# Fetching blocks of x with indirect gathers from GpSimd instead of plain transfers from SyncE

## The chip, the cores and the metric

The kernel runs on one core of a Trainium2 chip. The metric is the device time in microseconds (us) of one execution. A profile is one further execution, seen by the hardware profiler; its times are counted from the first instruction of its span. The engines are named as in the profile: PE is TensorE (PEld its weight loads), DVE is VectorE, ACT is ScalarE, POOL is GpSimd, SP is SyncE.

## What is computed

x has 16 blocks of 512 nodes with 128 features. A graph step and a mixture-of-experts step follow each other, each with a layer norm and a residual:

```python
def _layernorm(x): ...                      # over the last axis
def gnn(x):                                 # x is layernorm(x)
    h = x @ fc_in_w.T + fc_in_b
    for _ in range(8):
        h = h + 1/8 * (sigmoid(alpha) * 0.5 * (adj @ h - h) + h @ w_eff - h + x)
    return h
def moe(t):                                 # t is layernorm(x)
    p = softmax(t @ router_w.T)             # 8 experts, the 2 best, renormed
    return t + sum_e combine[:, e] * (gelu(t @ w1[e] + b1[e]) @ w2[e] + b2[e])
x = x + gnn(layernorm(x))
x = x + moe(layernorm(x))
```

## The kernel before

The 16 blocks are worked through as 8 groups of two blocks (GB = 2). The eight Euler steps are one polynomial in the node matrix and the feature matrix, worked out once at the start (up to about 57 us). Every fp32 operand of a matrix product is split in a high part (written by ACT) and a low part (written by DVE or POOL), and each product is three matmuls of these parts, `mm3`, lines 954 to 956.

Each engine has its own program, with semaphores between them. A loop body for group g holds two things: the graph step of group g, and after it the expert stage of group g - 1, with the first products of group g + 1 at its end. The first group has no expert stage (`iteration(0, first=True)`), then comes a hardware loop over groups 1 to 6, then `iteration(7, final=True)` and a last expert stage alone.

The expert stage has ITEMS = 16 items: two blocks by eight experts. Item i goes through the engines in this order: PE multiplies by w1 (the "up" product), ACT takes the gelu (line 494), DVE scales it by the routing weight (line 818, into `scaled`), ACT writes the high part into `scs` (line 397), POOL writes the low part (`item_low`, line 348), and PE multiplies by w2 (the "down" product), LAG = 5 items behind the up product. `scaled` has three slots, so DVE scales item i only after the low part of item i - 3 (line 817). `scs` has RING = 6 slots. Four of the 16 low parts, items 3, 4, 8 and 15 (`LOW_DVE`), are DVE's; the other 12 are POOL's. In the same stage DVE takes the statistics of the second layer norm (items 1 to 3), POOL takes the inverse root after item 2 (`inverse_root`, line 337), and DVE writes the normed z (line 579, items 6 to 8). PE transposes z at items 11 and 12.

POOL's order in a loop body: `residual(g - 1)` (line 355), the inverse root of the first layer norm of group g + 1, the sum of Q and xg (line 372), two low parts of x0 (line 342), then the low parts of the items with one inverse root among them. In the first group there are no items, and `residual(0)` is the next body's first instruction. DVE waits for it (`res_ready`, line 888) before its first sum of line 893.

x comes in as 256 KB transfers, one for each block of a group, into the one buffer `xn`. SP's `next_x(g)` waits until group g - 1 has been normed (`x0_ready`) and copied to `xg` (`xg_copied`), then issues two transfers (line 252). In a loop body it stands behind the replicated routing rows (`expert_weights`, line 286) and ahead of the stores of results (`store`, line 262). The data are read first by DVE's statistics of line 561 at the start of the next body.

## Time and profile before

| what | value |
|---|---|
| runs of the kernel before | 621.85 and 626.67 us, median 624.26 us |
| span of the profiled execution | 619.0 us |
| mean granted TensorE clock in it | 0.983 of full speed |
| length of one loop body | about 69.3 to 70.5 us, six of them |
| expert stage in it (group 3's body) | from 267.1 us to about 298.6 us |

The profile gives the span alone of the profiled execution, not its device time. The median of the runs is 5.3 us above the span, the two runs 2.9 and 7.7 us above it. Three views of the profile are used below. The timeline lists the instructions of one engine in order: start, duration, engine, line, operation, output<-input, and in brackets the idle time of the engine before it with what ended it. A group row ("x12 | 19.4, 1643") gives a count, the busy time in us and the mean of one in ns. A row by tile or line gives the shortest, median and longest duration in ns. An instruction's duration begins when it is issued to the engine, so that it holds time in which it is blocked.

### The profile page before, as it was taken

The numbers are of one execution on the slowest core, as the hardware profiler recorded it, in microseconds if no ns is written. First come the engines' busy times: TensorE is split into PE (matmuls) and PEld (weight loads), VectorE is DVE, ScalarE is ACT, GpSimd is POOL, SyncE is SP. The second block draws the span as 40 slices with busy tenths as digits, with TensorE's granted clock in tenths as the row PEclk, the third lists the DMA queues.
The fourth block names the chain that finished last, engine by engine and source line by source line (L and its number), as shares of the span: only waits on it lengthen the run. The fifth ranks groups of instructions, "written<-read, shape, count | busy, mean of one in ns | idle before, by whom it ended". The sixth has DMA issues, their size and how long they took to land.

```text
span 619.0 us, 9553 instructions
## 1 busy us (share of the span) xinstructions
PE 566.9 (92%) x3023; PEld 481.9 (78%) x3023; DVE 473.5 (76%) x1090; ACT 290.9 (47%) x477; POOL 250.2 (40%) x155
## 2 busy tenths in 40 slices
PE   3999999998999799998999799998999799998796
PEld 2778988976898588976898588976898588976574
DVE  5799776779676976779676976779676985579666
ACT  4322131367415662367415662367415672257574
POOL 2230320447213751447313761447313761147355
PEclk9999999999999999999999999999999989998899
DMA  5100010360105200250105300360105200350141
GB/s 181 35 0 1 0 35 1 107 202 1 34 2 210 95 17 17 104 203 0 34 2 197 107 17 17 104 203 0 34 2 191 80 17 19 104 171 0 43 164 35
DMA packets 25759, 43.15 MB, mean 70 GB/s; under 512 B 1462, under 2 KB 20236, under 8 KB 23820
## 3 DMA queue, kind: packets, MB, share of 16 engines
q1 hardware_dynamic: 25740, 42.91, 20.9%
q8 instruction: 10, 0.16, 0.1%
q14 instruction: 9, 0.07, 0.0%
HBM read 38.45 MB, written 4.46 MB: 69 GB/s over the span
## 4 chain that ended last, share of the span: by engine, by line
PE 63%; DVE 20%; issue 9%; ACT 3%; POOL 2%; DMA 1%; DVEq 0%; POOLq 0%; SPq 0%; ACTq 0%
PE bank L954 19%; PE bank L956 18%; PE bank L955 18%; DVE work L818 6%; DVE scr L579 3%; DVE bn L561 2%; PE bank L1080 2%; DVE scs L557 2%; POOL scs L348 2%; DVE x L579 2%; ACT work L494 2%; DVE mv L567 1%; PE bank L973 1%; PE bank L1094 1%; DMA work<-in_adj_dram 1%
## 5 line engine op out<-in xcount | busy, mean ns | idle before, releaser
L348 POOL TENSOR_TENSOR scs<-work,scs 128x512 fp32r<-128x512 f32 x96 | 153.1, 1617 | 103.5 <-ACT scs L397 103.3
L397 ACT ACTIVATE scs<-work 128x512 fp32r<-128x512 f32 (+1 forms) x129 | 82.8, 642 | 53.6 <-DVE work L818 52.3
L494 ACT ACTIVATE work<-bank,cols 128x512 f32<-128x512 f32 x128 | 86.8, 679 | 27.3 <-PE bank L956 27.0
L818 DVE TENSOR_TENSOR work<-work,GT 128x512 f32<-128x512 f32 x90 | 87.9, 990 | 9.6 <-ACT work L494 8.9
L337 POOL TENSOR_TENSOR rstd<-ve,nhalf 128x8 f32<-128x8 f32 x16 | 29.7, 1856 | 113.6 <-DVE ve L575 113.6
L954 PE MATMUL bank<-M,GT 128*128 128x384 f32 x192 | 65.6, 342 | 0.1
L955 PE MATMUL bank<-M,GT 128*128 128x384 f32 x192 | 65.0, 339 | 0.0
L956 PE MATMUL bank<-M,GT 128*128 128x384 f32 x192 | 65.0, 338 | 0.0
L557 DVE TENSOR_TENSOR GT<-bank,GT 128x512 fp32r<-128x512 f32 x48 | 32.2, 687 | 38.3 <-ACT GT L397 38.3
L954 PE MATMUL bank<-scs,w2s 128*128 128x512 f32 x128 | 56.3, 440 | 4.4 <-DVE scs L557 2.7
L397 ACT ACTIVATE GT<-bank 128x512 fp32r<-128x512 f32 x48 | 27.7, 594 | 67.5 <-PE bank L956 63.3
L397 ACT ACTIVATE scs<-Q 128x512 fp32r<-128x512 f32 x16 | 10.1, 632 | 94.1 <-DVE Q L893 94.1
L954 PE MATMUL bank<-LT,x0s 128*128 128x512 f32 x128 | 52.2, 408 | 1.8 <-DVE x0s L557 1.6
L954 PE MATMUL bank<-zT,w1s 128*128 128x512 f32 x128 | 53.8, 420 | 0.0
L955 PE MATMUL bank<-zT,w1s 128*128 128x512 f32 x128 | 51.8, 404 | 0.0
L956 PE MATMUL bank<-zT,w1s 128*128 128x512 f32 x128 | 51.7, 404 | 0.0
L955 PE MATMUL bank<-scs,w2s 128*128 128x512 f32 x128 | 51.4, 401 | 0.0
L956 PE MATMUL bank<-scs,w2s 128*128 128x512 f32 x128 | 51.3, 401 | 0.0
L956 PE MATMUL bank<-LT,x0s 128*128 128x512 f32 x128 | 51.3, 401 | 0.0
L893 DVE TENSOR_TENSOR Q<-bank,bias 128x384 f32<-128x384 f32 x64 | 35.5, 556 | 20.3 <-PE bank L956 19.5
L955 PE MATMUL bank<-LT,x0s 128*128 128x512 f32 x128 | 51.0, 398 | 0.0
L954 PE MATMUL bank<-scs,LT 128*128 128x256 f32 x128 | 36.7, 287 | 7.9 <-DVE scs L557 7.9
(188 smaller groups left out, 1382.1 us busy)
## 6 DMA issues: line engine op xcount, KB each, us to landing
GT<-comb_rows SPq DMA_DIRECT2D x8, 1536.0 KB, 6.8
Q<-comb_rows SPq DMA_DIRECT2D x16, 512.0 KB, 5.8
GT<-comb_rows SPq DMA_DIRECT2D x7, 1024.0 KB, 6.2
xn<-in_x_dram SPq DMA_DIRECT2D x16, 256.0 KB, 7.6
out_dram<-outs SPq DMA_DIRECT2D x16, 256.0 KB, 2.2
GT<-comb_rows SPq DMA_DIRECT2D x7, 512.0 KB, 4.3
work<-in_adj_dram SPq DMA_DIRECT2D x4, 256.0 KB, 5.4
Q<-in_L_ffn_w_dram SPq DMA_DIRECT2D x2, 512.0 KB, 5.9
```

The source lines that it names most:

```text
L337: nc.gpsimd.tensor_tensor(rstd[:, n, :], ve[:, n, :], nhalf[:, :], ALU.pow).then_inc(ln_rstd[n], 1)
L348: nc.gpsimd.tensor_tensor(scs[:, i % RING, 1, :], scaled[:, i % 3, :], scs[:, i % RING, 0, :].bitcast(FP32), ALU.subtract).then_inc(sc_lo_ ...
L397: return nc.scalar.activation(dst, src, ACT.Copy)
L494: nc.scalar.activation(hid[:, i % 2, :], bank[UP_BANK[i % 3]][:, :], ACT.Gelu, bias=cols[:, B1_COL + e:B1_COL + e + 1]).then_inc(gelu_done, 1)
L557: return v.tensor_tensor(dst, src, hi.bitcast(FP32), ALU.subtract)
L561: v.bn_stats(bn[:, n, t, :], src[:, t // GB, t % GB, :]).then_inc(ln_own[n], 1)
L579: return v.tensor_scalar(dst[:, t // GB, t % GB, :], src[:, t // GB, t % GB, :], mv[:, n, 0, t:t + 1], rstd[:, n, t:t + 1], ALU.subtract, ...
L818: v.tensor_tensor(scaled[:, i % 3, :], hid[:, i % 2, :], bank[REP_BANK[i % 2]][:, :] if by_pe else rep(i), ALU.mult).then_inc(sc_ready, 1)
L893: v.tensor_tensor(Q[:, :, t, b, :], src, bias[:, t], ALU.add).then_inc(q_ready, 1)
L954: pe.matmul(dst, wh, xh, start=start, stop=False)
L955: pe.matmul(dst, wh, xl, start=False, stop=False)
L956: return pe.matmul(dst, wl, xh, start=False, stop=stop)
```

## The change

All groups from 2 to 7 are fetched by POOL. Groups 0 and 1 still come by SP's plain transfers. A table of row numbers `x_row` (one column for each of the 8 tiles of 128 rows of a group) is written at the start; each `gather_x` is one indirect DMA that fetches 128 rows of 512 bytes, one to a partition, so a group is 8 gathers. In the first group all 8 stand behind the inverse root of line 337. In the loop bodies of groups 1 to 5 one stands behind each even item (0, 2, ..., 14), and behind item 0 there are also the addition that moves `x_row` on by a group (`next_rows`) and the two waits that were SP's. The body of group 6 is taken out of the loop, without gathers. DVE's statistics wait for the gathers' own semaphores.

```diff
@@ -86,6 +86,8 @@
+        x_row = sb("x_row", [P, NT, GB], I32)
+        x_step = sb("x_step", [P, NT, GB], I32)
@@ -164,6 +166,8 @@
+        rows_landed = [sem(f"rows_landed{b}") for b in range(GB)]
+        row_ready, gather_go = sem("row_ready"), sem("gather_go")
@@ -307,10 +311,8 @@
             next_x(1)
-            next_x(2)
             with sp.Fori(1, GROUPS - 2) as g:
                 expert_weights(g - 1, g)
-                next_x(g + 2)
                 store(g - 1)
@@ -329,7 +331,10 @@
             nc.gpsimd.memset(nhalf[:, :], -0.5).then_inc(pool_own, 1)
-            pool.wait_ge(pool_own, 2)
+            nc.gpsimd.iota(x_row[:, :, :], pattern=[[P, NT], [N, GB]], base=2 * GB * N,
+                           channel_multiplier=1)
+            nc.gpsimd.memset(x_step[:, :, :], GB * N).then_inc(pool_own, 1)
+            pool.wait_ge(pool_own, 3)
@@ -347,6 +352,25 @@
+            def next_rows(g):
+
+                for b in range(GB):
+                    pool.wait_ge(rows_landed[b], 16 * NT * (g - 2))
+                nc.gpsimd.tensor_tensor(x_row[:, :, :], x_row[:, :, :], x_step[:, :, :], ALU.add).then_inc(row_ready, 1)
+
+            def gather_x(g, k):
+
+                b, t = k // NT, k % NT
+                if k == 0:
+                    pool.wait_ge(x0_ready, g)
+                    pool.wait_ge(xg_copied, g)
+                    if not isinstance(g, int):
+                        pool.wait_ge(row_ready, g - 2)
+                    pool.sem_inc(gather_go, 1)
+                nc.gpsimd.indirect_dma_start(
+                    out=xn[:, t, b, :], out_offset=None, in_=x.rearrange("b n c -> (b n) c"),
+                    in_offset=bass.IndirectOffsetOnAxis(ap=x_row[:, t, b:b + 1], axis=0)).then_inc(rows_landed[b], 16)
@@ -362,7 +386,7 @@
-            def iteration(g, first=False, final=False):
+            def iteration(g, first=False, final=False, more=False):
@@ -374,16 +398,23 @@
                 if first:
                     inverse_root(1, g)
+                    for k in range(T):
+                        gather_x(g + 2, k)
                 else:
                     for i in range(ITEMS):
                         if i not in LOW_DVE:
                             item_low(g - 1, i)
                         if i == 2:
                             inverse_root(1, g)
+                        if more and i % 2 == 0:
+                            if i == 0:
+                                next_rows(g + 2)
+                            gather_x(g + 2, i // 2)
 
             iteration(0, first=True)
-            with pool.Fori(1, GROUPS - 1) as g:
-                iteration(g)
+            with pool.Fori(1, GROUPS - 2) as g:
+                iteration(g, more=True)
+            iteration(GROUPS - 2)
             iteration(GROUPS - 1, final=True)
@@ -580,7 +611,10 @@
             def norm_x_stats(g, b):
-                dve.wait_ge(x_in[b], 16 * g + 16)
+                if isinstance(g, int) and g < 2:
+                    dve.wait_ge(x_in[b], 16 * g + 16)
+                else:
+                    dve.wait_ge(rows_landed[b], 16 * NT * (g - 1))
```

## Rows read from the trace of the kernel before

**Rows 1.** Page, part 1: busy time, share of the span, instructions of each engine

```profile
PE 566.9 (92%) x3023; PEld 481.9 (78%) x3023; DVE 473.5 (76%) x1090; ACT 290.9 (47%) x477; POOL 250.2 (40%) x155
```

**Rows 2.** One body by stretches: length, PE, PEld, DVE, ACT, POOL busy, clock, DMA

```profile
239.00:270.20 31.20, 30.20 (x196) 28.80 (x196) 22.23 (x63) 11.04 (x19) 6.62 (x4) 1.00 0.25 89
270.20:296.50 26.30, 22.93 (x112) 17.25 (x111) 25.31 (x43) 19.27 (x33) 21.53 (x13) 1.00 0.22 75
296.50:309.00 12.50, 12.50 (x57) 10.09 (x56) 7.46 (x21) 4.75 (x9) 2.41 (x1) 1.00 0.14 42
```

**Rows 3.** Timeline of POOL in the expert stage: start, us, instruction, idle before

```profile
270.24 1.29 POOL L348 TENSOR_TENSOR scs<-work,scs 128x512 fp32r<-128x512 f32 x1 [9.30 <-ACT scs L397]
271.49 1.76 POOL L348 TENSOR_TENSOR scs<-work,scs 128x512 fp32r<-128x512 f32 x1
...
275.78 2.14 POOL L337 TENSOR_TENSOR rstd<-ve,nhalf 128x8 f32<-128x8 f32 x1 [0.83 <-DVE ve L575]
...
286.35 1.61 POOL L348 TENSOR_TENSOR scs<-work,scs 128x512 fp32r<-128x512 f32 x1 [1.94 <-ACT scs L397]
...
294.69 1.73 POOL L348 TENSOR_TENSOR scs<-work,scs 128x512 fp32r<-128x512 f32 x1
303.87 2.41 POOL L355 TENSOR_TENSOR scr<-Q,scr 128x1024 f32<-128x1024 f32 x1 [7.45 <-DVE outs L806]
```

**Rows 4.** Timeline of PE's weight loads: first and later down products, z's transposes

```profile
271.59 0.19 PEld L954 LDWEIGHTS bank<-scs,w2s 128*128 128x128 f32 x1 [0.27 <-POOL scs L348]
...
273.30 0.19 PEld L954 LDWEIGHTS bank<-scs,w2s 128*128 128x128 f32 x1 [0.47 <-POOL scs L348]
...
285.06 0.42 PEld L1094 LDWEIGHTS bank<-ident,scr 128*128 128x128 f32 x4 [3.10 <-DVE scr L579]
...
297.24 0.19 PEld L954 LDWEIGHTS bank<-scs,w2s 128*128 128x128 f32 x1
```

**Rows 5.** DVE: groups within 270.2 to 296.5, then shortest, median, longest over the span

```profile
L818 DVE TENSOR_TENSOR work<-work,GT 128x512 f32<-128x512 f32 x10 | 10.1, 1019 | 0.2 <-ACT work L494 0.2
L579 DVE TENSOR_SCALAR scr<-Q,mv,rstd 128x128 f32<-128x128 f32 x8 | 5.2, 699 | 0.0
...
L567 DVE TENSOR_TENSOR mv<-bn 128x8 f32<-128x8 f32 x1 | 1.3, 1259 | 0.0
...
L818 DVE TENSOR_TENSOR work<-work,GT x90: 674/693/1789, 129.0 to 606.3; 128x512 f32<-128x512 f32 x90
...
L579 DVE TENSOR_SCALAR x<-xn,mv,rstd x64: 335/341/2453, 10.6 to 464.3; 128x128 f32<-128x128 f32 x64
```

**Rows 6.** The transfers of x: SP's issue, and on the page KB and landing

```profile
268.45 1.06 SPq L252 DMA_DIRECT2D xn<-in_x_dram  x2
...
xn<-in_x_dram SPq DMA_DIRECT2D x16, 256.0 KB, 7.6
```

**Rows 7.** POOL: cheapest instruction, low parts of 270.2 to 296.5, inverse root

```profile
L331 POOL MEMSET nhalf<- 128x8 f32 x1 | 0.1, 102 | 0.0
...
L348 POOL TENSOR_TENSOR scs<-work,scs 128x512 fp32r<-128x512 f32 x12 | 19.4, 1643 | 13.1 <-ACT scs L397 13.1
...
L337 POOL TENSOR_TENSOR rstd<-ve,nhalf x16: 1642/1658/2138, 7.3 to 554.8; 128x8 f32<-128x8 f32 x16
```

**Rows 8.** Timelines of POOL, then DVE, behind the first group; last row a later body

```profile
86.96 1.65 POOL L337 TENSOR_TENSOR rstd<-ve,nhalf 128x8 f32<-128x8 f32 x1 [8.76 <-DVE ve L575]
90.98 2.36 POOL L355 TENSOR_TENSOR scr<-Q,scr 128x1024 f32<-128x1024 f32 x1 [2.37 <-DVE scr L579]
...
88.65 2.14 DVE L579 TENSOR_SCALAR scr<-Q,mv,rstd 128x128 f32<-128x128 f32 x8 [0.56 <-POOL rstd L337]
...
101.44 1.65 DVE L561 BATCH_NORM_STATS2 bn<-xn 128x6 f32<-128x128 f32 x8 [0.23 <-DVE rm L780]
...
103.60 0.55 DVE L893 TENSOR_TENSOR Q<-bank,bias 128x384 f32<-128x384 f32 x1
...
309.15 1.64 DVE L561 BATCH_NORM_STATS2 bn<-xn 128x6 f32<-128x128 f32 x8
```

## The prediction

> **What bounds the kernel now.** I read the page's busy times first. PE is busy 92% of the span and POOL 40% [rows 1]. That suggests that POOL has room, but it is an average over stages. The table by stretches shows where POOL's work lies: in a body of 70 us, 21.53 of its 30.56 us of busy time fall in the 26.30 us of the expert items, where it is 82% busy. DVE is busy 25.31 us of the same stretch and PE 22.93 [rows 2]. The gathers go into exactly this stretch.
>
> The timelines show who paces it. POOL's low part of item 0 ends at 271.53, and PE's waiting down product starts at 271.59. The next ends at 273.25, and PE starts at 273.30 [rows 3, 4]. So at its start POOL releases PE item by item. In the middle POOL idles briefly: 0.83 us for DVE before the inverse root, and 13.1 - 9.3 = 3.8 us for ACT before low parts [rows 3, 7], together about 4.65 us. PE waits 3.10 us for DVE's z [rows 4]. From 286.35 to 296.42 POOL works without a pause. Its last low part, item 14, ends at 296.42, and PE's down product of item 14 starts at 297.24 [rows 3, 4], only 0.82 us later.
>
> Last, I compared durations. A low part takes 1.29 us where it stands alone and 1.61 to 1.76 us where others precede it [rows 3]. DVE's scaling with two SBUF inputs takes 674 ns at best and 1,019 ns on average here; z's 128x128 scaling takes 699 ns on average here, where the same operation takes 335 ns elsewhere, and once 2,453 ns [rows 5]. Line 567, on 8 columns, took 1,259 ns [rows 5]. POOL and DVE hold each other up. DVE's excess is about (1.02 - 0.68) x 14 + (0.70 - 0.34) x 8 + 1.1 = 8.8 us per body.
>
> **What is removed.** SP's issue of 1.06 us per group, and a wait. SP next waits for stores that come much later, and nobody waits for x: its 7.6 us landing is over by about 277, and it is first read at 309.15 [rows 6, 8]. The removed part gives 0.
>
> **What is added, in a body with gathers.** POOL gets one addition on 128x8 integers, a few waits that are satisfied by then (SP's transfers, behind the same two waits, went out at 268.45 [rows 6]) and 8 gathers. The gather behind item 14 is followed by `residual`, which comes at 303.87 after 7.45 us of idling [rows 3], so it is hidden. Behind the other seven are queued low parts or the inverse root, which DVE's next scaling (through the three slots of `scaled`) and PE's down product wait for.
>
> The price D of one gather is the unknown: no POOL transfer is in this trace. From below there is POOL's cheapest instruction, 0.10 us [rows 7]. SP's issue of two larger transfers takes 1.06 us, so 0.53 each [rows 6]. From above there is the inverse root on only 8 columns, 1.66 to 2.14 us [rows 7], which shows what POOL's software costs where each element needs many steps. A gather reads 128 row numbers and writes out 128 rows' addresses by software, so I put it nearest to an undisturbed low part, D = 1.3 us [rows 3]. For the range I keep 0.1 and 2.1.
>
> The Trainium skill, "DMA: Bandwidth & Descriptors", section "Latency and other measured facts", puts GpSimd's first byte at about 1 us against 0.6 us for SyncE's. No row here shows it. By D = 1.0 the sum below would give about +2 us instead of +15.
>
> **The sum for one body.** I start at the end of item 0's low part, 271.53, and lay POOL's work end to end, since with gathers it has almost no pause left. The addition takes 0.2. Of the 11 low parts left, six follow a gather or one and meet DVE less (a gather gives DVE time): 6 x 1.29 = 7.7. Five follow another low part: 5 x 1.72 = 8.6. The inverse root takes 2.1. Seven gathers take 7 x 1.3 = 9.1. That is 27.7 us, and item 14 ends at 299.2 in place of 296.4. PE took it at 297.24, so PE is 2.0 us later. To this I add 0.5 us for pauses that stay (between 0 and the 4.65 us of idling there are now), most of the old idle time being filled. The result is +2.5 us per body. In this sum one tenth of a microsecond in D is 0.7 us per body. At D = 0.95 the whole is hidden.
>
> Everything behind item 14 (out, the first products of the next group, the next body) follows PE, so the 2.5 us aren't given back. PE, 87% busy in the stretch, can't make them up. Five bodies give 5 x 2.5 = 12.5 us.
>
> **The first group.** Eight gathers start at 88.6 and take 10.4 us, to 99.0. `residual` is queued behind them and moves from 90.98 to 99.0, ending at 101.4 [rows 8]. DVE needs it at 103.60, a cover of 2.2 us that is gone at D = 1.57. The last rows must land for the second half of DVE's statistics at 102.3 (101.44 plus half of 1.65). With the quickest landing of x in the trace (2.6 us) they come at 101.6. DVE's eight scalings of z start at 88.65 [rows 8], just when the gathers start, and may be blocked as above. I add 1.5 us for the group, between 0 and 8 (each scaling behind one gather at worst). The rest costs nothing: the two new setup instructions are as small as the cheapest row [rows 7] and stand at the start, where POOL waits for DVE's first statistics.
>
> Sum: 12.5 + 1.5 = 14, with half a microsecond of loop and semaphore instructions on POOL about 15 us. The profiled span would go from 619.0 to 634, and the median of runs, 5.3 us above the span, from 624.3 to 639.
>
> **Rivals.** *The gathers are hidden* (chance 0.30). If D is about 1.1 us or less, POOL's old pauses and its blocked time take them in. For it speaks that POOL idles 4.65 us in the stretch and is blocked for about 12 x (1.643 - 1.29) = 4.2 us [rows 7]. Against it speaks that seven gathers at 1.1 are 7.7 us and that the end has 0.82 us of slack. It gives 5 x (0 to 1) = 0 to 5 us, so 621 to 630.
>
> *The gathers cost more than a low part, or shut DVE out* (0.25). DVE is 96% busy in the stretch, and the line 579 rows show that it can be held for a whole POOL instruction. At D = 1.8 the sum gives 7 x 0.5 = 3.5 us more per body, and 2.1 + 2.4 - 2.2 = 2.3 us more in the first group: 639 + 17.5 + 2.3 = 659. At 2.1 it gives 5 x 5.6 + 6 = 34 more, 673.
> The Trainium skill, "SBUF — State Buffer", section "SBUF: two separate sides", warns of this pair: while DVE runs a copy or scaling in its two-port mode, GpSimd can't write descriptors, and it advises SyncE's path for such transfers. The rows agree that the two exclude each other, 2,453 ns for 335; how a gather fares no row shows. By that rule eight scalings of z per body lengthen gathers by up to 8 x 0.34 = 2.7 us, so up to 13 us in all, about 652.
>
> *Faster* (0.03). DVE is the busiest engine of the stretch and loses 8.8 us to POOL. If gathers are cheap (below about 0.5 us, so that 7 x 0.5 fits in the old pauses) and leave DVE's inputs alone, they spread the low parts and DVE's scalings run unblocked. The bound is PE's idle time of the stretch, 26.30 - 22.93 = 3.4 us per body, so at most 5 x 3.4 = 17 us: 607. Against it: the low parts stay as many and as long, and only a third of the cover would appear.
>
> *x comes late* (0.02 alone). The last gather would go out at about 299.2 to 300.5 and is needed, shifted by the same delay, at 311. It would need over 10 us to land, where 512 KB now take 7.6 [rows 6]. Then DVE would wait, and the next products behind it: over 3 us a body.
>
> **How the numbers follow.** The forecast, D of 1.1 to 1.6 and POOL pacing the items, has 0.40 and spans 630 to 652. The likeliest value is 639. The range leaves out the dearest part of the second rival and the faster case: 621 to 664. A change of 2%, 12.5 us, is about what a measurement of this kernel can tell from no change. Slower by over 2% (above 636.7) holds most of the forecast (0.26 of its 0.40), the second rival and the late landing, together 0.53. Within 2% holds the hidden case, the rest of the forecast and a little of the faster one: 0.45. Faster by over 2% has 0.02.
>
> **What would show it.** In the changed profile each gather has a busy time on POOL; I expect 1.3 us, and low parts behind a gather near 1.3, others near 1.7. The expert stretch of POOL, first to last low part, should grow from 26.2 to about 29, and a body with gathers from 69.5 or 70.4 to 72 or 73, while the body of group 6 stays. PE's waits for POOL's low parts should grow, now at items 13 and 14 too. DVE's mean for lines 818 and 579 should fall if gathers leave it alone, and rise if they block it. SP should show no more waits for xg. The forecast is wrong if D is outside 1.1 to 1.6, if DVE's z becomes what PE waits for longest, or if the bodies grow after item 14.

## The result, and the profile after

The changed kernel takes 655.3 us (median), the kernel before 624.3 us: a ratio of 1.053, 95% interval 1.046 to 1.060. The profiled span is 651.1 us, where it was 619.0. The change costs 31 us by the medians and 32 by the spans, where 15 were forecast. Each ratio below compares with runs of the kernel before that were taken beside it, and leaves out the few runs, of either kernel, that were over 1.5% longer than the fastest of their kernel.

The page, parts 1, 3 and 5 (part 5: instructions | busy us, mean ns | idle before, releasers):

```profile
PE 582.3 (89%) x3023; PEld 494.9 (76%) x3023; DVE 496.3 (76%) x1090; ACT 291.9 (45%) x477; POOL 295.4 (45%) x210
...
q0 software_dynamic: 1536, 3.15, 1.6%
...
L353 POOL TENSOR_TENSOR scs<-work,scs 128x512 fp32r<-128x512 f32 x96 | 139.7, 1475 | 88.3 <-ACT scs L428 87.6
...
L371 POOL DMA_INDIRECT xn<-in_x_dram,x_row x48 | 55.1, 1147 | 13.2 <-issue 7.8
```

POOL has 45 us more busy time [rows 1]: the gathers add 48 x 1,147 ns = 55.1 us, the low parts take 13.4 less, and the additions make up the rest. The 1,536 packets are their 6 x 8 x 32.

The body of the same group by stretches, as in [rows 2] (length, PE, PEld, DVE, ACT, POOL busy, clock, DMA):

```profile
251.90:283.10 31.20, 30.20 (x197) 28.81 (x196) 22.24 (x63) 11.07 (x19) 6.64 (x4) 1.00 0.25 86
283.10:314.00 30.90, 24.98 (x104) 19.33 (x103) 29.66 (x43) 19.11 (x33) 27.49 (x21) 0.86 0.20 65
314.00:326.50 12.50, 12.50 (x56) 10.15 (x55) 6.49 (x17) 3.94 (x7) 3.72 (x3) 0.93 0.15 47
```

Nearly all the growth is in the item stretch: 26.3 us became 30.9, POOL's work went from 21.5 to 27.5 us and DVE's from 25.3 to 29.7, though DVE has the same 43 instructions. The third row is a window of the same length in both kernels, so it shows only what is in it. The granted clock fell to 0.86 in the item stretch and to 0.93 behind it.

POOL's timeline of this stretch, to be laid beside [rows 3]:

```profile
283.14 1.29 POOL L353 TENSOR_TENSOR scs<-work,scs 128x512 fp32r<-128x512 f32 x1 [9.27 <-ACT scs L428]
284.39 0.65 POOL L360 TENSOR_TENSOR x_row<-x_row,x_step 128x8 int32<-128x8 int32 x1
285.95 1.30 POOL L371 DMA_INDIRECT xn<-in_x_dram,x_row  x1 [0.91 <-POOL x_row L360]
287.28 2.50 POOL L353 TENSOR_TENSOR scs<-work,scs 128x512 fp32r<-128x512 f32 x2
290.25 2.17 POOL L342 TENSOR_TENSOR rstd<-ve,nhalf 128x8 f32<-128x8 f32 x1 [0.47 <-DVE ve L606]
...
295.29 2.52 POOL L353 TENSOR_TENSOR scs<-work,scs 128x512 fp32r<-128x512 f32 x2
...
305.68 1.25 POOL L371 DMA_INDIRECT xn<-in_x_dram,x_row  x1
306.95 2.56 POOL L353 TENSOR_TENSOR scs<-work,scs 128x512 fp32r<-128x512 f32 x2
...
310.93 3.15 POOL L353 TENSOR_TENSOR scs<-work,scs 128x512 fp32r<-128x512 f32 x2
314.23 1.23 POOL L371 DMA_INDIRECT xn<-in_x_dram,x_row  x1 [0.16 <-issue]
```

Behind three of the seven gathers (those of items 0, 4 and 10) two low parts run back to back in 2.5 us. Behind item 2's comes the next gather, behind item 6's one low part, and behind those of items 8 and 12 DVE still gets in between (1.60 + 1.73 and 1.47 + 1.72 us). DVE's timeline at the same times, and then PE's weight load for the logits (the router's product of z, line 1114), show what the pairs do:

```profile
286.63 3.18 DVE L602 TENSOR_TENSOR mv<-mv 128x8 f32<-128x8 f32 x1
...
294.37 3.79 DVE L610 TENSOR_SCALAR scr<-Q,mv,rstd 128x128 f32<-128x128 f32 x3
...
306.82 3.25 DVE L852 TENSOR_TENSOR work<-work,GT 128x512 f32<-128x512 f32 x1
309.99 0.68 DVE L588 TENSOR_TENSOR zT_next<-bank,zT_next 128x512 fp32r<-128x512 f32 x1
```

```profile
310.72 0.30 PEld L1114 LDWEIGHTS bank<-rts,zT 128*128 128x128 f32 x2 [1.06 <-DVE zT_next L588]
```

Each of the first three rows holds an instruction that is not done before the second low part of a pair ends (289.78, 297.81, 309.51). The second row is three scalings of z, one of which takes 3.28 us. All three instructions had started 0.1 to 0.6 us before the end of the gather ahead of the pair. But a scaling that started at 310.59, 0.3 us before the end of item 12's gather, took its usual 0.67 us; what decides is open. The last of the three holds up z's low part (line 588), and PE's logits wait for that. Before, the same places read as follows, in rows of DVE and PEld not shown ahead of the prediction:

```profile
290.74 1.18 DVE L818 TENSOR_TENSOR work<-work,GT 128x512 f32<-128x512 f32 x1
291.89 0.69 DVE L557 TENSOR_TENSOR zT_next<-bank,zT_next 128x512 fp32r<-128x512 f32 x1
```

```profile
292.63 0.30 PEld L1080 LDWEIGHTS bank<-rts,zT 128*128 128x128 f32 x2 [0.46 <-DVE zT_next L557]
```

Three marks cut a body well: item 0's low part, z's first transpose on PE, the logits. These are worked out from the timelines, for the bodies with gathers, "+" counted from the mark before. A body is counted from one `residual` to the next; the first does not compare, as the first group's gathers move the `residual` that it starts with from 91 to 99 us.

| kernel | to z's transposes | to the logits | to the residual | body | DVE's longest scaling |
|---|---|---|---|---|---|
| before | +14.8 | +7.6 or 8.7 (clock 1.00 or 0.80) | +11.2 | 69.3 to 70.4 (first 73.1) | 1.79 |
| after | +17.8 | +9.75 (clock 0.80 to 0.83) | +11.2 (12.8 and 14.4 in two) | 74.1 to 77.7 | 3.25 |

The last leg is the same 11.2 us wherever the clock is full in it. So everything from the logits on only follows, and a body grows by what delays the logits: 27.6 us behind item 0's low part, where it was 22.4 or 23.5. Item 14's low part does not set this leg. In the body of group 2 it ends at 239.60, 3.4 us behind the logits, and PE comes to its down product 4.6 us behind them, as before, and without a wait:

```profile
240.83 0.19 PEld L988 LDWEIGHTS bank<-scs,w2s 128*128 128x128 f32 x1
```

That is a slack of 1.23 us, where it was 0.82 or 1.84 before. The body of group 6, without gathers, takes 70.3 us, for 70.8 before.

### The profile page after: what moved, and what is told of

Its sections match the earlier page's. It is cut to its first block, busy times and chain, and to the rows that moved or that the text cites. A ratio compares the mean times of both kernels' runs of the same rounds, so it can differ in the third digit from the quotient of the medians.

```text
span 651.1 us, 9567 instructions
## 1 busy us (share of the span) xinstructions
PE 582.3 (89%) x3023; PEld 494.9 (76%) x3023; DVE 496.3 (76%) x1090; ACT 291.9 (45%) x477; POOL 295.4 (45%) x210
## 3 DMA queue, kind: packets, MB, share of 16 engines
q1 hardware_dynamic: 19404, 39.76, 17.8%
q0 software_dynamic: 1536, 3.15, 1.6%
## 4 chain that ended last, share of the span: by engine, by line
PE 61%; DVE 18%; issue 12%; ACT 5%; POOL 2%; DMA 1%; another core or an unknown queue 0%; DVEq 0%; SPq 0%; POOLq 0%; ACTq 0%
PE bank L988 18%; PE bank L989 17%; PE bank L990 17%; DVE work L852 5%; DVE scr L610 3%; ACT work L525 2%; DVE bn L592 2%; DVE scs L588 2%; PE bank L1114 2%; POOL scs L353 2%; DVE x L610 1%; PE bank L1128 1%; PE bank L1007 1%; ACT scs L428 1%; DMA work<-in_adj_dram 1%
## 5 line engine op out<-in xcount | busy, mean ns | idle before, releaser
L353 POOL TENSOR_TENSOR scs<-work,scs 128x512 fp32r<-128x512 f32 x96 | 139.7, 1475 | 88.3 <-ACT scs L428 87.6
L852 DVE TENSOR_TENSOR work<-work,GT 128x512 f32<-128x512 f32 x90 | 96.5, 1085 | 10.4 <-ACT work L525 9.5
L988 PE MATMUL bank<-scs,w2s 128*128 128x512 f32 x128 | 59.6, 466 | 21.9 <-POOL scs L353 21.0
L588 DVE TENSOR_TENSOR GT<-bank,GT 128x512 fp32r<-128x512 f32 x48 | 32.3, 687 | 43.2 <-ACT GT L428 41.1
L371 POOL DMA_INDIRECT xn<-in_x_dram,x_row x48 | 55.1, 1147 | 13.2 <-issue 7.8
L428 ACT ACTIVATE GT<-bank 128x512 fp32r<-128x512 f32 x48 | 27.7, 594 | 68.1 <-PE bank L990 61.8
L988 PEld LDWEIGHTS bank<-scs,w2s 128*128 128x128 f32 x128 | 26.7, 208 | 37.6 <-POOL scs L353 30.7
L988 PE MATMUL bank<-zT,w1s 128*128 128x512 f32 x128 | 55.2, 431 | 0.0
L988 PE MATMUL bank<-LT,x0s 128*128 128x512 f32 x128 | 52.4, 409 | 2.5 <-DVE x0s L588 2.1
L989 PE MATMUL bank<-scs,w2s 128*128 128x512 f32 x128 | 54.3, 424 | 0.0
L990 PE MATMUL bank<-scs,w2s 128*128 128x512 f32 x128 | 53.7, 420 | 0.0
L990 PE MATMUL bank<-zT,w1s 128*128 128x512 f32 x128 | 53.4, 417 | 0.0
L989 PE MATMUL bank<-zT,w1s 128*128 128x512 f32 x128 | 53.2, 415 | 0.0
L989 PE MATMUL bank<-LT,x0s 128*128 128x512 f32 x128 | 51.0, 398 | 0.0
```

Of the source, the lines that this page charges most:

```text
L353: nc.gpsimd.tensor_tensor(scs[:, i % RING, 1, :], scaled[:, i % 3, :], scs[:, i % RING, 0, :].bitcast(FP32), ALU.subtract).then_inc(sc_lo_ ...
L371: nc.gpsimd.indirect_dma_start(out=xn[:, t, b, :], out_offset=None, in_=x.rearrange("b n c -> (b n) c"), in_offset=bass.IndirectOffsetOnAx ...
L428: return nc.scalar.activation(dst, src, ACT.Copy)
L588: return v.tensor_tensor(dst, src, hi.bitcast(FP32), ALU.subtract)
L852: v.tensor_tensor(scaled[:, i % 3, :], hid[:, i % 2, :], bank[REP_BANK[i % 2]][:, :] if by_pe else rep(i), ALU.mult).then_inc(sc_ready, 1)
L988: pe.matmul(dst, wh, xh, start=start, stop=False)
```

## The experiments

Lines of code are those of the changed kernel. "Row addition early" means that `next_rows` stands behind `residual`, a body's first instruction on POOL.

### Is it the addition, or where the gathers stand?

**rows_early** moves only the addition and its waits.

```diff
                     residual(g - 1)
+                if more:
+                    next_rows(g + 2)
...
-                            if i == 0:
-                                next_rows(g + 2)
```

> The changed kernel with only the addition on the row numbers moved: it stands behind `residual`, where POOL idles for over 11 us, in place of behind item 0's low part. In the changed kernel that spot costs POOL 0.65 us of addition and 0.91 us until the first gather starts. Theory A, POOL's own time between the low parts sets the body: the 1.56 us come off each of five bodies, 7.8 us in all, so a ratio to the kernel before near 1.040 in place of 1.053. Theory B, PE's long wait there is made by the gather and not by the addition, or the 1.56 us fall into slack: no more than 2 us come off, ratio 1.050.

Measured: 656.2 us, 1.050 (1.042 to 1.058). The addition and the wait behind it, 0.65 + 0.91 us above, are gone, and yet the first leg fell only from 17.8 to 17.45 us and the second not at all, 2 us over five bodies, as theory B has it. The ratio by itself could not tell. Behind the logits all five bodies are at a lowered clock, 12.8 to 14.5 us for 11.2, which costs 11.2 us together, where after loses 4.8. DVE was shut out sooner, and the inverse root waited for it instead:

```profile
213.16 1.28 POOL L371 DMA_INDIRECT xn<-in_x_dram,x_row  x1 [0.16 <-issue]
214.47 2.51 POOL L353 TENSOR_TENSOR scs<-work,scs 128x512 fp32r<-128x512 f32 x2
218.43 2.18 POOL L342 TENSOR_TENSOR rstd<-ve,nhalf 128x8 f32<-128x8 f32 x1 [1.45 <-DVE ve L606]
```

This run also tells what makes the second leg 9.75 us long. PE in that leg of two bodies (length, busy, clock, DMA):

```profile
229.14:238.88 9.74, 8.93 (x37) 0.82 0.04 13
306.39:316.13 9.74, 7.37 (x37) 1.00 0.04 13
```

Three of the five bodies have the full clock in it, and PE waits 2.6 us for z's low part; two have the lower clock, and PE waits 1.0 us. The length is the same. So the low part on DVE sets it, and the clock is not needed for it.

**gathers_last** puts all eight behind item 14's low part, row addition early.

```diff
-                        if more and i % 2 == 0:
-                            gather_x(g + 2, i // 2)
+                    if more:
+                        for k in range(T):
+                            gather_x(g + 2, k)
```

> As rows_early, and all eight gathers of a body stand behind item 14's low part, where POOL idled 7.45 us before `residual`. Same transfers, same POOL work, other place. Theory A: the bodies are back at 69.3 to 70.4 us and only the first group's 3 us stay, ratio 1.00 to 1.01. Rival, the fetch itself is what costs (transfers of 512 bytes, x that lands late, or DVE held up by gathers wherever they stand): over 2 us per body stay, ratio 1.02 or more.

Measured: 628.0 us, 1.007 (1.003 to 1.011). Nearly all of the cost goes with the place. The body is 70.2 us from the second on, the longest scaling 1.79 us, the first leg is 14.8 us as before. `residual` is queued behind the gathers (13.0 to 14.0 us behind the logits for 11.2), which the body does not feel. The eight take 10 us, an idle POOL's price:

```profile
231.90 1.29 POOL L371 DMA_INDIRECT xn<-in_x_dram,x_row  x1 [0.17 <-issue]
233.49 0.95 POOL L371 DMA_INDIRECT xn<-in_x_dram,x_row  x1 [0.30 <-issue]
...
241.96 2.41 POOL L379 TENSOR_TENSOR scr<-Q,scr 128x1024 f32<-128x1024 f32 x1
```

### POOL's time, or what a gather does beside it?

**memsets** is the kernel before with seven pauses in the places of the gathers, in six bodies. x comes by SP, and there is no addition. The longer memset writes `outs`, so two waits, not shown, keep it and the results apart.

```diff
+            def pause(g, n):
+                nc.gpsimd.memset(outs[:, :, :, :], 0.0).then_inc(paused, 1)
+                nc.gpsimd.memset(spare[:, :], 0.0).then_inc(paused, 1)
+                pool.wait_ge(paused, 14 * (g - 1) + 2 * n)
...
+                        if not final and i % 2 == 0 and i < 14:
+                            pause(g, i // 2 + 1)
```

> The kernel before, x by SP, with seven pauses on POOL in each of six bodies, behind the low parts of items 0, 2, ... 12 (at item 2 ahead of the inverse root): a memset of 1,024 columns (about 0.95 us), one of 48 columns, and a wait for both, about 1.2 us against a gather's 1.17 busy and 0.2 of gap. They write and read nothing that DVE's operations need. The addition is not in it. Theory A, only POOL's time counts: 7 x 1.2 us as in rows_early, so about the same growth per body as there, some 3 us, 18 us over six bodies, ratio 1.03. Theory C, a gather is dearer than its time, because POOL's low parts behind it hold the shared inputs from early on and shut DVE out: the pauses cost under half of that, ratio 1.01, and DVE's mean for its scaling stays near 1.02 us where the gathers raised it to 1.19.

Measured: 641.7 us, 1.026 (1.018 to 1.034). A pause is 0.95 + 0.13 us and a wait, about 1.25 us. DVE's longest scaling stays at 1.78 us. The first leg is 17.2 to 17.5 us, as in rows_early; the second is 8.6 to 9.9, and PE never waits in it: its clock is 0.80 or 0.69. A body grows by 3.6 us in all; the logits of after alone come 5.2 us later. So up to z's transposes the pauses, with no scaling of an item held over 1.78 us, cost what the gathers do. POOL's time is enough for the first leg. What the gathers add is in the second.

**plain8** issues eight plain transfers of 64 KB from POOL in the same places, **plain2** two of 256 KB behind items 0 and 2, both without row numbers.

```diff
-                nc.gpsimd.indirect_dma_start(
...
+                pool.dma_start(xn[:, t, b, :], of_group(x_v, g, b)[:, t, :]).then_inc(rows_landed[b], 16)
```

> The changed kernel with plain transfers issued by POOL in place of the gathers: eight of 64 KB at the same places, no row numbers and no addition. If the cost is that POOL writes the transfer's descriptors by software at all, a plain one costs POOL nearly what a gather costs (1.17 us busy and 0.16 to 0.30 of gap) and the ratio is 1.045 to 1.05, as in rows_early. If the cost is in looking up the row numbers, a plain one is under 0.6 us and the ratio is under 1.015.

> As plain8 with two transfers of 256 KB in place of eight of 64 KB, behind item 0 and behind the inverse root of item 2. The same bytes in rows of 512 bytes, so the same number of rows to write descriptors for. If POOL's cost is per instruction: two of about 1.2 us, of which the pauses take most, ratio 1.00 to 1.01. If it is per row: each takes about four times a plain8 transfer's time, in two lumps, ratio 1.04 or more.

Measured: plain8 629.8 us, 1.012 (1.007 to 1.016); plain2 624.0 us, 1.001 (0.998 to 1.004). Group rows of plain8, then of plain2:

```profile
L362 POOL DMA_DIRECT2D xn<-in_x_dram x48 | 27.0, 564 | 0.0
```

```profile
L362 POOL DMA_DIRECT2D xn<-in_x_dram x12 | 9.7, 805 | 0.0
```

A plain transfer takes 0.56 us with no gap; an indirect one of the same bytes 1.15 and a gap of 0.16 to 0.30. The first leg of plain8 grows by 0.95 us; four transfers of 0.56 are over by then. The longest scaling is 2.70 us in plain8 and 2.62 in plain2: low parts run in pairs behind a plain transfer too.

### Which place binds?

By the forecast's model the low part of item 14 paces the body. The rival (called E in the expectations) says that the logits do, behind z's low part on DVE. Four runs place the gathers accordingly, row addition early in all:

```diff
-                        if more and i % 2 == 0:
+                        if more and i in (0, 2, 4, 6, 8, 10):   # no12, two more behind item 14
+                        if more and i in (0, 4, 8, 12):         # half, four more behind item 14
+                        if more and i in (10, 12):              # late, six more behind item 14
...
+                        for k in (0, 1, 2, 3, 4):               # split, ahead of item 0, three behind item 14
+                            gather_x(g + 2, k)
```

> The row addition stands behind the residual, gathers stand behind items 0, 2, 4, 6, 8 and 10 and the last two behind item 14's low part; the one behind item 12 is so taken out of the item stretch. Model of the prediction (item 14's down product is what the low parts delay): item 14's low part comes 1.35 us earlier in each of five bodies than with the gather behind item 12, and the five bodies shorten by that: 1.050 - 5 x 1.35 / 624 = 1.039. Theory E (the body is paced by the logits, which wait for z's low part on VectorE, some 2 us after item 11's low part and ahead of what item 12's gather delays): nothing is gained, 1.046 to 1.052, and the start of item 0's low part to the logits stays at 27.2 us.

> Gathers behind items 0, 4, 8 and 12 only, four more behind item 14's low part, row addition behind the residual. Three gathers are left ahead of the logits in place of six. Theory E with a growth in proportion: the stretch from item 0 to the logits grows by 2.0 to 2.7 us instead of 4.8, so 1.020 to 1.026. A theory of slack (some microseconds of POOL time are free, the rest is paid in full): 3 x 1.35 less 0.8 and less what the low parts quicken would leave 1 to 2 us a body: 1.009 to 1.017.

> No gather between low parts: five stand ahead of item 0's low part, where POOL waits 9.3 us for the kernel's first scaled product, and three behind item 14's; row addition behind the residual. Theory E and the model of the prediction alike: nothing is paid for POOL's time, only the first group's part, 1.000 to 1.008. The rival, that a gather costs by its traffic or by the port it shares wherever it stands: 1.02 or more.

> Gathers behind items 10 and 12, six more behind item 14's low part, row addition behind the residual. Against the run with all eight behind item 14 (1.007) it adds two gathers among the last low parts. Model of the prediction (item 14's down product is what they delay, with 0.8 us of slack): 2.7 us less what the low parts quicken (0.4) less 0.8 is 1.5 us a body, 1.007 + 0.012 = 1.019. Theory E (what is ahead of z's low part and the logits paces the body): 1.005 to 1.010, and item 0 to the logits stays within 0.5 us of 22.4.

| kernel | ratio (interval) | to z's transposes | to the logits | body | longest scaling |
|---|---|---|---|---|---|
| rows_early | 1.050 (1.042 to 1.058) | +17.45 | +9.7 | 75.5 to 77.3 | 3.42 |
| no12 | 1.044 (1.037 to 1.051) | +17.4 | +9.75 | 72.7 to 77.2 | 3.39 |
| half | 1.018 (1.011 to 1.025) | +16.8 | +8.5 to 9.9 | 71.0 to 73.3 | 3.59 |
| split | 1.017 (1.010 to 1.024) | +15.7 | +8.7 | 70.6 to 72.0 | 3.24 |
| late | 1.016 (1.008 to 1.023) | +14.8 | +9.8 | 70.1 to 71.6 | 3.52 |

*no12*: the gather behind item 12 gone, the logits come 27.2 us behind item 0, as in rows_early. That leg confirms E. But item 14's low part, too, ends at 30.5 us in both, since POOL waits for ACT ahead of item 13's:

```profile
387.00 3.28 POOL L353 TENSOR_TENSOR scs<-work,scs 128x512 fp32r<-128x512 f32 x2 [1.30 <-ACT scs L431]
```

So the 1.35 us that the forecast's model takes off did not arise, and the run doesn't test that step. By the ratio alone neither is excluded: 1.039 and 1.046 to 1.052 both touch the interval. The low clock behind the logits costs 8.0 us here and 11.2 in rows_early, which is about what the ratios differ by.

*late*: the ratio lies between the two expectations, and E's second claim, the logits within 0.5 us of 22.4, failed: they come at 24.7. Item 10's gather is ahead of the logits after all. DVE and PEld of this run:

```profile
224.78 3.47 DVE L855 TENSOR_TENSOR work<-work,GT 128x512 f32<-128x512 f32 x1
228.17 0.68 DVE L591 TENSOR_TENSOR zT_next<-bank,zT_next 128x512 fp32r<-128x512 f32 x1
```

```profile
228.91 0.30 PEld L1117 LDWEIGHTS bank<-rts,zT 128*128 128x128 f32 x2 [1.28 <-DVE zT_next L591]
```

This one gather pairs the low parts of items 11 and 12, and DVE's scaling ahead of z's low part is blocked for both. It is the plainest case. The first leg is that of before, and the scaling starts 20.5 us behind item 0, as before. It takes 3.3 to 3.5 us for 1.0 to 1.2, and the logits come 2.3 us later than at full clock before. In half, with no gather behind item 10, that scaling takes 0.7 to 1.1 us, and PE never waits for z's low part in a body with gathers.

*half*: the ratio lies between the two expectations. z's transposes come 2.0 us later, with two gathers (items 0 and 4) over by the time of DVE's last scalings of z. Four such gathers cost 2.6 us there (no12), four plain transfers 0.95, plain2's two 0.57, five pauses 2.4 to 2.7. For each microsecond of POOL's time, gaps included, that is 0.4 to 0.8 us. So none of it was free, and the cost isn't in proportion to POOL's time alone. The logits come 2.9 to 4.3 us later than 22.4, a microsecond or more of it by the clock (0.80 or 0.69 in the second leg, in which PE doesn't wait).

*split* missed both ways of telling: 1.017 with no gather between low parts. POOL's and DVE's timelines show why:

```profile
204.39 1.40 POOL L371 DMA_INDIRECT xn<-in_x_dram,x_row  x1 [0.30 <-issue]
205.81 2.52 POOL L353 TENSOR_TENSOR scs<-work,scs 128x512 fp32r<-128x512 f32 x2
```

```profile
205.67 3.23 DVE L856 TENSOR_TENSOR work<-work,GT 128x512 f32<-128x512 f32 x1
```

The gathers start only at 199.3 us, so the fifth runs 0.7 us into the time of item 0's low part (36.4 us behind the residual instead of 35.7), and the pair behind it shuts DVE out.

### Taking the fifth gather away, and the pair apart

**four_ahead** has four gathers ahead of item 0 and four behind item 14. **spaced** is rows_early with a short memset behind each gather in the items.

```diff
-                        for k in (0, 1, 2, 3, 4):
+                        for k in (0, 1, 2, 3):                  # four_ahead
...
+                            nc.gpsimd.memset(spare[:, :], 0.0)  # spaced, behind each gather
```

> Four gathers ahead of item 0's low part and four behind item 14's, in place of five and three; row addition behind the residual. The four end at about 204.3 us where item 0's product is there at about 205.1, so nothing holds item 0's low part: the stretch from the residual to item 0 returns from 36.4 to 35.7 us, the stretch from item 0 to z's transposes from 15.7 to 14.8 us, and 1.0 to 1.6 us a body goes: 1.003 to 1.009. The rival, that the gathers ahead of item 0 cost by themselves (the x it brings comes to SBUF while TensorE and VectorE work): 1.012 or more.

> The run with the row addition behind the residual (1.050), with a memset of 32 columns put between each of the seven gathers in the item stretch and the low part behind it. Theory P (the body grows by POOL's time alone): seven memsets of some 0.13 us add up to 0.9 us a body, 1.050 to 1.058, whether or not VectorE is shut out. Theory L (about 0.8 us or more of a body's growth is VectorE shut out while two low parts follow each other at 1.26 us): if the memset restores the low parts' usual 1.6 to 1.7 us with a scaling of VectorE between them, VectorE's longest scaling falls from 3.4 us to below 2 us, and the time falls to 1.035 to 1.046. If the low parts keep their 1.26 us behind the memset, nothing is decided.

four_ahead: 633.9 us, 1.018 (1.013 to 1.023), so the ratio missed. The marks came as expected: residual to item 0 35.7 us, first leg 14.8, longest scaling 1.78 us. The loss is in the second leg, 10.0 us in every body, also in group 6's, which has no gathers. Stretches of PE from z's transposes to the logits (length, busy, clock), of four_ahead and then of two bodies of before:

```profile
220.80:230.80 10.00, 10.00 (x38) 0.69 0.00 0
```

```profile
285.06:292.60 7.54, 7.36 (x37) 1.00 0.00 0
...
214.60:223.30 8.70, 8.69 (x37) 0.80 0.00 0
```

PE works all the time in it. The same 37 or 38 operations take 7.5 us at the full clock, a wait of 0.46 us among them, 8.7 at a mean of 0.80 and 10.0 at 0.69. So the clock alone, between its levels of 2.4 and 1.2 GHz, moves this leg by 2.5 us. Which bodies get it is not tied to a gather in them, and memsets, which has none at all, is at 0.69 to 0.71 in three. Why this kernel has it in every body is open, so its ratio doesn't exclude the rival.

spaced: 654.4 us, 1.052 (1.050 to 1.055). POOL's and DVE's rows:

```profile
210.15 1.28 POOL L374 DMA_INDIRECT xn<-in_x_dram,x_row  x1 [0.16 <-issue]
211.44 0.15 POOL L418 MEMSET spare<- 128x32 f32 x1
211.53 2.52 POOL L356 TENSOR_TENSOR scs<-work,scs 128x512 fp32r<-128x512 f32 x2
```

```profile
211.25 3.36 DVE L858 TENSOR_TENSOR work<-work,GT 128x512 f32<-128x512 f32 x1
```

The memset does not break up the pair, so this run does not tell what the shut-out is worth, as its expectation says.

### The first group, and the clock

**first_only** keeps the gathers in the first group alone. **early_filler** is rows_early with 8 more matmuls in PE's wait ahead of item 1's down product. **before_filler** is the kernel before with 10 more ahead of z's transposes. The extra matmuls write a bank that is not read.

```diff
+                    if s == 6 and g is not None:                # early_filler
+                        for _ in range(8):
+                            pe.matmul(bank[3][:, :], w1s[:, 0, 0, :], zT[:, 0, 0, :], start=True, stop=True)
```

> The kernel before, with gathers for group 2 alone, in the first group as in the changed kernel; groups 3 to 7 by SP. It prices the first group by itself: the changed profile has its next body 3.0 us later there, while the eight gathers end before `residual` is wanted. If these 3 us belong to the gathers: ratio 1.005, and the same idle time of 3 us ahead of the router's first sum on DVE. If they were chance or belong to the changed loop: ratio 1.000.

> rows_early with eight extra matmuls of 512 columns on PE in each body but the first, between the up product of item 6 and the down product of item 1, where PE waits 2.0 to 2.5 us for POOL's low part. They write a bank that nobody reads then; about 1.9 us of work inside the wait. Theory D, part of the loss is TensorE's clock: rows_early's tails (item 14's low part to `residual`) took 9.4 to 11.1 us where 7.4 to 7.9 is seen at full clock, because PE's long pauses are followed by stretches at half clock. With the pause filled the clock stays up, the item stretch stays at 30.5 us (POOL sets it) and the tails fall to about 8: some 2 to 3 us off each of five bodies, ratio 1.03 in place of 1.050. Rival: the tails are long because POOL is late, and extra work on PE can only cost: ratio 1.05 or more.

> The kernel before with ten extra matmuls of 512 columns on PE ahead of the transposes of z (item 11), where PE waits 3.10 us for DVE; about 2.3 us of work inside that wait, written to a bank that nobody reads then. In the kernel before every second body has about 3.4 us at half clock in its item stretch and a tail of 8.46 us in place of 7.45. Theory D: with the wait filled these spells go, 1.0 us comes off three or four bodies, ratio 0.993 to 0.995. If the spells have another cause: 1.000, or up to 1.01 where the extra work pushes PE back.

Measured: first_only 622.0 us, 0.997 (0.994 to 1.000); early_filler 652.3 us, 1.047 (1.041 to 1.053); before_filler 622.6 us, 1.001 (0.998 to 1.003). In neither kernel did work in one of PE's waits bring the clock back. In before_filler the half clock left the item stretch and came behind it instead, two tails of 9.0 us for 7.4. In early_filler the tails stay at 7.9 to 11.05 us.

The first group's gathers in the changed kernel, beside [rows 8], and DVE's first sum of the router:

```profile
88.81 1.26 POOL L371 DMA_INDIRECT xn<-in_x_dram,x_row  x1 [0.19 <-issue]
...
97.91 0.94 POOL L371 DMA_INDIRECT xn<-in_x_dram,x_row  x1 [0.30 <-issue]
98.87 2.42 POOL L379 TENSOR_TENSOR scr<-Q,scr 128x1024 f32<-128x1024 f32 x1
```

```profile
100.39 0.29 DVE L794 TENSOR_REDUCE rt<-bank 128x64 f32<-128x128 f32 x1 [3.17 <-remote]
```

`residual` ends at 101.3, as forecast for D of 1.3. Item 0 of the first body comes at 134.10 instead of 130.45, 3.65 us late; in other kernels without gathers there it comes at 129.3 to 130.2. The wait of 3.2 us shows in six of the eleven kernels with these gathers (after, rows_early, gathers_last, first_only, four_ahead, spaced) and not in the other five (early_filler, no12, half, split, late), which reach item 0 at 132.2 to 132.8 (split, whose gathers hold it, at 133.8). In these five the delay has a row. `residual` now runs from 98.5 on, beside DVE's work on the router, and one instruction of that takes 2.18 us, for 0.23 before (late's row):

```profile
98.84 2.18 DVE L808 TENSOR_TENSOR rt<-rt,rm 128x64 f32<-128x64 f32 x1
```

With the wait of 3.2 us, item 0 comes at 133.5 to 134.4. Its releaser is not in the profile and its cause is open. first_only has the wait and comes 3.1 us late to item 0 too, and yet its span is that of before, 618.8 us. Its bodies are each about 0.6 us shorter from `residual` to item 0 (35.1 us for 35.7), and no run shows why. So its ratio of 0.997 does not show that the first group's gathers are free.

## Where the prediction held and where it failed

**Direction and place held.** The kernel is slower; the item stretch of the bodies with gathers grew, group 6's body did not, and SP and the landing of x play no part.

**The price of a gather held.** Forecast 1.3 us. Measured in the items 1.02 to 1.35 us and a gap of 0.14 to 0.30. On an idle POOL it is 0.95 + 0.30 = 1.25 us. Low parts in the pairs behind a gather take 1.27 to 1.31 us; with POOL's group mean at 1,475 ns (1,643 in [rows 7]) they are even quicker than expected.

**The sum of POOL's work was 1.5 us short a body.** It gave 27.7 + 0.5 from the end of item 0's low part to the end of item 14's. Measured: 314.08 - 284.43 = 29.65. The addition was put at 0.2 us and took 0.65 + 0.91 of wait for its result, 1.36 more. The 12 low parts are busy 16.6 us, 11 of them 15.3 instead of 16.3; the pauses that stayed were about 1.3 instead of 0.5, and the gathers with their gaps 9.3 instead of 9.1. rows_early shows that the addition's excess is not the cause of the miss: gone, it gives back 0.4 us a body. Two sums beside the main one are off as well. At D = 1.8 the first group comes to 8 x 0.5 - 2.2 = 1.8 us, not 2.3. At D = 1.0 the whole comes to about +4 us with the sum's own 1.5 and 0.5, not +2.

**The step that failed is the one that takes off 0.82 us of slack at item 14's down product** and lets 2.0 us reach PE, with everything behind item 14 following from there. Item 14's low part came 4.8 us later and still had 1.23 us of slack, more than the 0.82. What paces the body is the logits, which wait for z's low part on DVE. [rows 4] do not show that row. It had 0.46 us of PE waiting in the body that the forecast read, so no slack at all. (In every second body, at the lower clock, PE did not wait for it.) The mark to look for was the last wait ahead of a leg of fixed length (the 11.2 us from the logits to the residual), not the last item.

Measured growth at full clock before: 3.0 us to z's transposes and 2.2 from there to the logits, 5.2 us for 2.5 forecast. Of the 3.0, 0.4 is the addition. The other 2.6 come from what POOL does ahead of item 8; memsets shows that POOL's time is enough for them, and half that they don't follow it in proportion. The 2.2 are the blocked scaling ahead of z's low part (3.25 for 1.18 us). late has them with an unchanged first leg, and rows_early has them at the full clock as at 0.82. The low clock alone can make the leg as long (four_ahead), but here it falls into PE's wait and adds nothing.

**DVE shut out was a rival with 0.25, and a part of it happened.** It was tied to a dearer gather (D of 1.8). The gather was not dear; what follows it was. The forecast expected that "a gather gives DVE time" and took quick low parts behind one as good news. In the pairs they are quick while DVE does not get in between them. Of the two means that it said would "rise if they block it" (lines 818 and 579, now 852 and 610, in the item stretch) this came true: 1,019 to 1,188 ns, 699 to 882 ns:

```profile
L852 DVE TENSOR_TENSOR work<-work,GT 128x512 f32<-128x512 f32 x10 | 11.8, 1188 | 0.3 <-ACT work L525 0.2
L610 DVE TENSOR_SCALAR scr<-Q,mv,rstd 128x128 f32<-128x128 f32 x8 | 6.6, 882 | 0.0
```

The rule weighed there (the Trainium skill, "SBUF — State Buffer", section "SBUF: two separate sides") had DVE hold up the gather. The runs show that small, 1.02 to 1.40 us for 0.95 and once 2.84 (in spaced). Large was the other direction, POOL's low parts holding DVE. The page says that whichever of the two starts first has the shared ports for its whole instruction. DVE's rows here had started first, and outlast two of POOL's instructions.

**The clock was left out.** Its mean is 0.950 over the span, 0.983 before. Two bodies of after have the lower clock behind the logits, 12.8 and 14.4 us for 11.2, 4.8 us together. That is one of the forecast's own signs, bodies that grow after item 14. Before, two of the five bodies had it between z's transposes and the logits, at 1.1 us each, which the longer waits of after swallow.

**The first group was put at 1.5 us and cost about 3.65.** Kernels without the unexplained wait on DVE put it at 1.8 to 2.3 us (132.2 to 132.8 for 130.45). The step there looked only at when DVE needs the result of `residual`; its 2.4 us beside DVE's router work, which hold DVE up by 1.95, were left out. The rest came with that wait.

Together: 5 x 5.2 = 26.0 for the logits, less 2.2 for before's own slow legs, 4.8 for the clock behind the logits, 3.65 for the first group: 32.3, where the span grew by 32.1.

## What to carry to other kernels

Cut a loop body at its last wait ahead of a stretch of fixed length, and count slack there; an engine's last low part can have slack that is worth nothing. Software-issued DMAs between the elementwise instructions of a POOL that DVE shares its inputs with can cost twice: about 1.3 us of POOL each, and a DVE instruction blocked where two low parts follow at once. Put them where POOL has nothing queued behind (1.007 here), or issue a few large plain ones (1.001); none of the placements in the loop was faster than SyncE's plain transfers.

## What was not expected of the hardware

- Where two 128x512 subtractions of POOL follow at once behind a DMA that POOL issued, they mostly take 1.26 to 1.31 us each, and an instruction of DVE with two SBUF inputs, or a scaling of z, waits for both: 3.0 to 3.6 us behind an indirect DMA, 2.4 to 2.95 behind a plain one. An instruction on 8 columns waited as long, 3.18 us. Behind a memset with a wait for its result the two take 1.27 and 1.75 us, or 2.0 and 1.28, and DVE's longest scaling is 1.78 us. A memset with no such wait, put between DMA and pair, changes nothing. The Trainium skill, "GPSIMD Engine Reference", section "Instruction dispatch", says that the cores of POOL are not held together between instructions, each starting the next when its own share is done. That would fit cores that run apart behind a DMA and together again behind a wait; no run here shows single cores.
- An indirect DMA of 128 rows of 512 bytes takes an otherwise idle POOL 0.94 us and leaves 0.30 us until the next; a plain one of the same bytes 0.56 us with no gap, one of four times the bytes 0.80.
- An integer addition of 128x8 takes 0.20 us on an idle POOL, 0.65 us among low parts, and 0.91 us pass until an indirect DMA that uses the result starts.
- Extra matmuls in a wait of PE moved the half clock elsewhere, and gained nothing in either kernel.
